# Attention with two heads per quarter of 32 partitions, score products on four row tiles, and five batches in flight

## The chip, the cores and the metric

The kernel runs on one core of one Trainium2 chip. The core has five engines that run their own instruction streams: TensorE (PE, products; its weight loads are shown as PEld), VectorE (DVE), ScalarE (ACT), GpSimd (POOL) and SyncE (SP, which here only starts DMAs). They meet at semaphores. The metric is the device time of one execution of the whole program in microseconds, the median of the runs; lower is better.

## The reference, cut to what matters

The program is a small audio tower over 64 sequences of 256 x 128: a convolution to tokens (64 x 248 x 64), an attention layer, a feed-forward layer on the top half of the tokens, a recurrent layer with fast weights, and a layer of experts. The change is in the attention layer, which for each batch of 248 tokens and 64 channels computes, with 8 heads of 8 channels:

```python
q, k = heads of x @ Wqk.T;  v = heads of x @ Wv.T
patch = softmax(einsum('bhnd,bhmd->bhnm', q, k) * 8 ** -0.5)
pos   = softmax(rel(n, m) @ Wpos.T + bpos)          # the same for every batch
attn  = (1 - sigmoid(gating)) * patch + sigmoid(gating) * pos
out   = (attn / attn.sum(-1)) @ v
h_att = h_tok + heads joined(out) @ Wproj.T + bproj
```

x is the normed h_tok. Both are scratch tensors in HBM, of 64 x 124 x 2 x 64 floats.

## The kernel before, in words

`attention_layer` (line 250) first sets up its constants, among them `rt`, the 8 position softmaxes (lines 363 to 366, 493 to 496 and 532 to 549). Then every engine runs a loop over the 64 batches, one batch per iteration, with the first and last batch written out. The order on each engine is the order in the code; `Loop` (line 21) turns a named event of batch n into a value of a semaphore.

The 248 tokens stand as two halves of 124 (TL) on partitions. A batch goes like this on TensorE:

- Eight score products (line 438). All 64 channels of q are the weights (124 tokens) and `ka` holds, for each head, the keys with all other heads' channels set to zero, two heads per product: 496 moving columns. VectorE takes the maximum over the keys of each (line 615). The scores use two banks in turn, so product i waits for maximum i-2. Between them stand three parts of the batch before: its sums are turned (line 414) and VectorE normalizes them (lines 586 to 599), the attended values are turned (421) and projected (427), and VectorE adds h_tok (610).
- The weighted sums of the position weights (line 393 with `rt`): per head 32 output partitions, so four heads share the array as column tiles of 32.
- The maxima are turned into rows (line 449) and VectorE copies them, negated, under the queries (`qa`, line 624): the maximum is subtracted by the product itself, by 8 extra rows of `ka` that pick the head.
- Eight times two turned score products (line 458): keys are the weights, `qa` moves, 248 columns each, all 128 rows in use. ScalarE takes the exponential (line 506) into `ex`. Again two banks, so head h waits for exponential h-2.
- The next batch's x is turned (373), copied by VectorE (558), multiplied to queries and keys (378); VectorE scales the queries (561) and spreads the keys over the heads (565: 64 partitions x 1984 elements). ScalarE copies the queries (509).
- The weighted sums of `ex` (line 393 again; line 392 waits for one exponential ahead of each product of the first half), then the values of the next batch (383). VectorE copies the sums (634) and the values (569). The next batch's score products wait for that last copy (line 432).

SP loads x and h_tok of a batch and stores its result (lines 330 to 354), each with one buffer. All of it is fp32; each product runs as two passes, which are two records in the trace.

Elsewhere in the kernel, the recurrent layer has other products in tiles. Line 2277 multiplies 32 rows by 128 columns, alternating two quarters of the rows and two banks, and the full products of line 2290 and the column tiles of lines 2303 and 2310 follow it. Their code is:

```python
for w in range(2):
    for k in range(2):
        rows = slice(32 * g, 32 * g + 32)          # g differs with k
        mm = e.matmul(psNew[X % 2][k][:, HD * w:HD * w + HD], wy[rows, ...], hist[rows, m * 4 + j, 0:HD], start=True, stop=True)
```

Of the kernel before, what the change touches and what calls it, by code (L numbers as in the profile page):

```python
# [7 lines left out]
ALU = mybir.AluOpType  # L8
ACT = mybir.ActivationFunctionType
AX = mybir.AxisListType.X  # L10
# [239 lines left out]
def attention_layer(nc, Wqk, Wv, Wpos, bpos, Wproj, bproj, gating, H0, X0, H1):  # L250
# [5 lines left out]
    with ExitStack() as ctx:  # L256
# [3 lines left out]
        wT = S.sb("wT", [D + 1, 4, D])  # L260
        prm = S.sb("prm", [TL, 40])
        hm = S.sb("hm", [D, NH])
# [5 lines left out]
        xT = S.sb("xT", [D, L])  # L268
# [3 lines left out]
        mx = S.sb("mx", [TL, 2, NH])  # L272
        ex = S.sb("ex", [TL, NH, 2, L])
# [6 lines left out]
        V = Loop(S.sem("vector"), [f"mx{i}" for i in range(8)] + ["nm", "xT", "q", "k", "evs", "v"])  # L280
        VE = Loop(S.sem("vector_end"), ["rz", "rzg", "num", "rv", "sum", "rd", "at0", "at1", "aT", "h1"])
        A = Loop(S.sem("scalar"), ["rvs"] + [f"e{h}" for h in range(NH)] + ["qc"])
        T = Loop(S.sem("tensor"), [f"s{i}" for i in range(8)] + ["rv", "nm"] + [f"st{h}" for h in range(NH)] +
                 ["xT", "qk", "ev", "v"])
        TE = Loop(S.sem("tensor_end"), ["te", "tr", "aT", "pr"])
        xin = Loop(S.sem("x_in"), ["x"], 16, 0)
        s_x0, s_t0, s_v0, s_a0 = S.sem("first_x_in"), S.sem("first_tensor"), S.sem("first_vector"), S.sem("first_scalar")
        hin = Loop(S.sem("h_in"), ["h"], 16, 0)
        out = Loop(S.sem("out"), ["h"], 16, 0)
        with nc.Block() as block:  # L290
            @block.gpsimd
            def _(e):
# [3 lines left out]
                e.memset(hm[:, :], 1.0).then_inc(s_id, 1)  # L296
                e.wait_ge(s_id, 3)
                e.memset(ka[D:, :, :], 1.0).then_inc(s_id, 1)
                e.wait_ge(s_id, 4)
                e.memset(va[:, :, :, :], 0.0).then_inc(s_id, 1)  # L300
                e.wait_ge(s_id, 5)

                e.affine_select(out=hm[:, :], in_=hm[:, :], compare_op=ALU.is_ge, fill=0.0, base=0,
                                pattern=[[-8, NH]], channel_multiplier=1).then_inc(s_id, 1)
                e.wait_ge(s_id, 6)
                e.affine_select(out=hm[:, :], in_=hm[:, :], compare_op=ALU.is_ge, fill=0.0, base=7,
# [15 lines left out]
            def _(e):  # L322
# [11 lines left out]
                def store(n):  # L334
                    VE.wait(e, n, "h1")
                    settled(e, s_own_sp)
                    e.dma_start(row(H1, n), h1[:, :, :]).then_inc(out.sem, 16)
# [2324 lines left out]
```

## Time and profile before

| | |
|---|---|
| median of 3 runs | 11612.14 us (11609.99 to 11624.89) |
| the profiled execution | 11640.99 us |
| its span, first to last instruction | 11639.3 us |
| mean granted TensorE clock over the span | 0.872 |
| PE busy, share of the span | 9361.1 us, 80% |
| DVE busy | 4926.0 us, 42% |
| ACT busy | 1971.5 us, 17% |

The granted clock is a fraction of 2.4 GHz. An engine is busy while one of its instructions runs; products are pipelined, their records overlap, and so the start of one record to the start of the next tells more than their lengths. "Idle before" is the time in which an engine had nothing to run ahead of a group, and what ended it. Numbers of one profiled execution are not the times of the unprofiled runs: here the former is 28.85 us longer than the median.

### The profile page before, as it was taken

How to read it: one execution, taken by the hardware profiler on the slowest of the kernel's cores; microseconds unless marked ns; L12 is line 12 of the kernel's file. 1: busy time of each engine (PE TensorE's matmuls, PEld its weight loads, DVE VectorE, ACT ScalarE, POOL GpSimd, SP SyncE). 2: the span in 40 equal slices, each digit the busy share in tenths (PEclk: the TensorE clock that was granted, in tenths of full speed). 3: DMA queues.
4: the chain of work that ended last, by engine and by line, in shares of the span. 5: the costliest groups of instructions: out<-in, count | busy, mean ns of one | idle time of the engine just before them, and what ended most of it. 6: DMA issues, size and time to landing. Idle time of an engine off the chain costs nothing. (4 is left out here: it accounts for less than half of the span.)

```text
span 11639.3 us, 367698 instructions
## 1 busy us (share of the span) xinstructions
PE 9361.1 (80%) x150364; PEld 5949.8 (51%) x150364; DVE 4926.0 (42%) x12504; ACT 1971.5 (17%) x4398; POOL 232.7 (2%) x167
## 2 busy tenths in 40 slices
PE   5788886242568988988989988989889898986777
PEld 2455553112346766666666666657566575652222
DVE  3444444544744344334344343333333333335555
ACT  1222221122111011011011011110111101113333
POOL 0000000000100000000000000000000000000000
PEclk8899998555889989989999989879789797887888
DMA  2000000142621011011021011120221202210000
GB/s 58 6 8 8 7 8 15 37 131 41 123 74 57 19 56 57 19 56 57 19 57 56 20 56 57 49 86 19 86 60 46 86 20 85 64 43 12 11 11 10
DMA packets 894544, 521.49 MB, mean 45 GB/s; under 512 B 379950, under 2 KB 889462, under 8 KB 892534
## 3 DMA queue, kind: packets, MB, share of 16 engines
q1 hardware_dynamic: 880694, 502.37, 15.9%
q0 software_dynamic: 13312, 12.57, 0.6%
q8 instruction: 262, 4.29, 0.2%
q14 instruction: 276, 2.26, 0.1%
HBM read 323.24 MB, written 154.20 MB: 41 GB/s over the span
## 5 line engine op out<-in xcount | busy, mean ns | idle before, releaser
L2344 PE MATMUL bank<-mv,hdiag 128*32 128x144 f32 x63744 | 2082.2, 289 | 9.8 <-DVE hdiag L2513 8.3
L2344 PEld LDWEIGHTS bank<-mv,hdiag 128*32 128x32 f32 x63744 | 1954.0, 111 | 95.1 <-DVE hdiag L2513 12.3
L2379 PE MATMUL bank<-mvt,ydiag 128*32 128x256 f32 x31872 | 1955.2, 381 | 0.0
L2379 PEld LDWEIGHTS bank<-mvt,ydiag 128*32 128x32 f32 x31872 | 1086.5, 110 | 533.6 <-issue 2.9
L438 PE MATMUL att_bank<-att_ka,att_qn 128*124 128x496 f32 x1024 | 496.2, 597 | 133.6 <-DVE att_mx L615 67.0
L2545 DVE TENSOR_TENSOR rep<-bank,ta 128x128 f32<-128x128 f32 x249 | 72.7, 292 | 1220.5 <-PE bank L2344 1220.5
L2223 ACT ACTIVATE work<-work 128x128 f32<-128x128 f32 x498 | 154.1, 309 | 2413.9 <-DVE work L2503 2413.9
L2468 DVE SCALAR_TENSOR_TENSOR mvt<-mvt,cu,bank 128x256 f32<-128x256 f32 x512 | 223.2, 477 | 741.6 <-PE bank L2277 741.6
L2277 PE MATMUL bank<-hist,wy 32*128 32x256 f32 x2048 | 399.6, 559 | 169.4 <-DVE wy L2458 169.4
L2211 ACT ACTIVATE mv<-bank 128x256 f32<-128x256 f32 x1024 | 325.1, 385 | 1100.7 <-PE bank L2290 1100.5
L458 PE MATMUL att_bank<-att_qa,att_ka 128*124 128x248 f32 x2048 | 464.6, 385 | 32.6 <-DVE att_qa L624 32.6
L1554 DVE TENSOR_TENSOR moe_hw<-moe_hb,moe_bank 128x496 f32<-128x496 f32 x512 | 326.2, 669 | 323.6 <-ACT moe_hb L1413 297.0
L2290 PE MATMUL bank<-r_ident,mvt 128*128 128x128 f32 x2048 | 404.2, 362 | 34.7 <-DVE mvt L2476 34.0
L2576 DVE TENSOR_SCALAR work<-bank,ta 128x128 f32<-128x128 f32 x498 | 174.9, 351 | 591.7 <-PE bank L2379 591.7
L458 PEld LDWEIGHTS att_bank<-att_qa,att_ka 128*124 128x124 f32 x2048 | 345.9, 186 | 144.3 <-DVE att_qa L624 48.8
L1335 PE MATMUL moe_bank<-moe_x,moe_w 128*128 128x496 bf16 x1536 | 412.4, 412 | 0.0
L2277 PEld LDWEIGHTS bank<-hist,wy 32*128 32x128 f32 x2048 | 232.5, 264 | 349.3 <-issue 248.2
L615 DVE TENSOR_REDUCE att_mx<-att_bank 124x2 f32<-124x496 f32 x512 | 339.0, 672 | 166.5 <-PE att_bank L438 162.7
L2290 PEld LDWEIGHTS bank<-r_ident,mvt 128*128 128x128 f32 x2048 | 320.8, 187 | 168.5 <-issue 99.9
L2310 PE MATMUL bank<-hdiag,ct 128*32 128x256 f32 x2944 | 317.8, 542 | 108.7 <-DMA hdiag<-between_slopes 108.7
L1413 ACT ACTIVATE moe_hb<-moe_bank,moe_b1s 128x496 f32<-128x496 f32 x512 | 328.7, 670 | 268.1 <-PE moe_bank L1335 262.2
L506 ACT ACTIVATE att_ex<-att_bank 124x496 f32<-124x496 f32 x512 | 298.5, 583 | 223.3 <-PE att_bank L458 223.3
(402 smaller groups left out, 10682.5 us busy)
## 6 DMA issues: line engine op xcount, KB each, us to landing
hdiag<-between_slopes SPq DMA_DIRECT2D x368, 512.0 KB, 4.7
baset<-between_base SPq DMA_DIRECT2D x265, 128.0 KB, 2.1
between_base<-work SPq DMA_DIRECT2D x256, 128.0 KB
hist<-h SPq DMA_DIRECT2D x1992, 8.0 KB
hist<-y SPq DMA_DIRECT2D x1992, 2.0 KB
hist<-dl SPq DMA_DIRECT2D x1992, 8.0 KB
ct<-between_table SPq DMA_DIRECT2D x184, 128.0 KB, 3.7
between_slopes<-key_zero SPq DMA_DIRECT2D x8, 2048.0 KB
```

The costliest lines, as they stand in the source:

```text
L438: e.matmul(bank[3 + i % 2][0:TL, 0:2 * L], qn[:, TL * a:TL * a + TL], ka[:, 2 * hp:2 * hp + 2, :], start=True, stop=True).then_inc(T.sem, 1)
L458: mm = e.matmul(bank[3 + h % 2][0:TL, L * mh:L * mh + L], ka[:, h, TL * mh:TL * mh + TL], qa[:, :], start=True, stop=True)
L615: e.tensor_reduce(mx[:, i // 4, 2 * (i % 4):2 * (i % 4) + 2], bank[3 + i % 2][0:TL, 0:2 * L].rearrange("p (h m) -> p h m", h=2), AX, ALU.m ...
L1335: mm = e.matmul(bank[2 + 2 * a + q][:, 0:2 * L], w[:, x_, 128 * a:128 * a + 128], xp[:, 2 * L * q:2 * L * q + 2 * L], start=(k == 0), stop ...
L1413: e.activation(hb[:, a, q, :], bank[2 + 2 * a + q][:, 0:2 * L], ACT.Relu, bias=b1s[:, x_, a:a + 1]).then_inc(A.sem, 1)
L1554: e.tensor_tensor(hw[:, a, q, :], hb[:, a, q, :], bank[q][:, 0:2 * L], ALU.mult).then_inc(V.sem, 1)
L2211: e.activation(dst, src, ACT.Copy).then_inc(A.sem, 1)
L2277: mm = e.matmul(psNew[X % 2][k][:, HD * w:HD * w + HD], wy[rows, G % 2, w, :, :].rearrange("p u d -> p (u d)"), hist[rows, m * 4 + j, 0:HD ...
L2290: mm = e.transpose(psC[k][:, o:o + 128], mvt[:, 4 * n + j, HD * w + 128 * hf:HD * w + 128 * hf + 128], ident[:, :])
L2310: mm = e.matmul(out[rows, :], ct[:, yk % 2, 1 + k, g % 2, rows], ring[xk % DX][:, j, :], start=False, stop=(k == nb - 1))
L2344: mm = e.matmul(psP[32 * j:32 * j + 32, 0:MW], hdiag[:, hf, r, j, :], mv1[:, hf, r, j, :], start=(hf == 0 and r == 0), stop=(hf == 1 and r ...
L2379: mm = e.matmul(psBack[hf][32 * j:32 * j + 32, :], ydiag[:, n, j, :], both, start=(n == 0), stop=(n == 7))
```

## The change: what it does

The layout of the heads changes. Partitions 32g to 32g+32 (a quarter) now hold heads 2g and 2g+1: 16 rows of channels, then 2 rows for the two maxima. The weights for queries and keys (`wqk`) are spread to this layout in the setup, with a row of ones for the maxima's rows of the keys, so queries and keys come out of one product each with 128 outputs. `ka` holds for each quarter the keys of its first and its second head, 2 x 248 columns on 128 partitions. A score product uses the 32 rows of one quarter as weights and moving data; so does a turned one. The maxima are written to where a transposing product brings them under the right rows, and VectorE forms `qa` by one subtraction.

Score product i goes to quarter i mod 4 and banks 0 and 1; the turned products of step i use quarter (i + 2) mod 4 and banks 2 and 3 (`TILE_HEAD` gives the head).

The order changes. There is one body, a turn k, of eight steps. In it: the scores and maxima of batch k+1, the turned scores and exponentials of k, the weighted sums of k-1 (in steps 4 to 7), the sums' turning and normalizing of k-2, the end of k-3, and x, queries, keys of k+2 with their values at the end of the turn. `qn`, `ka`, `va` and `ex` have three buffers. The loop holds three turns and runs 19 times; turns -2 to 2 and 60 to 66 are written out, without the parts whose batch does not exist. ScalarE takes over the copies of the sums, the values, x and the attended values. Each stage has a semaphore of its own.

```diff
-        qn, qa, ka = S.sb("qn", [128, L]), S.sb("qa", [128, L]), S.sb("ka", [128, NH, L])
-        va = S.sb("va", [TL, 2, NH, 32])
+        qn, ka = S.sb("qn", [128, 3, L]), S.sb("ka", [128, 3, 2, L])
+        qa = S.sb("qa", [128, L])
+        va = S.sb("va", [TL, 3, 2, NH, 32])
+        mx = S.sb("mx", [TL, 2, 128])
+        ex = S.sb("ex", [TL, 3, NH, 2, L])
...
+        TILE_HEAD = [2 * ((i + 2) % 4) + i // 4 for i in range(8)]
...
+        def turns(e, body):
+            for k in range(-2, 3):
+                body(Turn(k, k % 3))
+            with e.Fori(0, 19) as m:
+                for u in range(3):
+                    body(Turn(3 * m + (3 + u), u))
+            for k in range(60, B + 3):
+                body(Turn(k, k % 3))
...
+                def score(t, i):
+                    a, g = i // 4, i % 4
+                    rows = slice(32 * g, 32 * g + 32)
+                    if i == 0:
+                        t.wait(e, V_in, 1, "ka")
+                    t.wait(e, V_max, 1 if i >= 2 else 0, f"mx{(i - 2) % 8}")
+                    e.matmul(bank[i % 2][0:TL, 0:2 * L], qn[rows, t.buf(1), TL * a:TL * a + TL], ka[rows, t.buf(1), :, :],
+                             start=True, stop=True).then_inc(T_max.sem, 1)
+
+                def score_turned(t, i):
+                    h = TILE_HEAD[i]
+                    rows = slice(32 * (h // 2), 32 * (h // 2) + 32)
+                    if i == 0:
+                        t.wait(e, V_max, 0, "qa")
+                    t.wait(e, A_exp, 0 if i >= 2 else -1, f"e{(i - 2) % 8}")
+                    for mh in range(2):
+                        mm = e.matmul(bank[2 + i % 2][0:TL, L * mh:L * mh + L], ka[rows, t.buf(0), h % 2, TL * mh:TL * mh + TL], qa[rows, :],
+                                      start=True, stop=True)
+                    mm.then_inc(T_exp.sem, 1)
+
+                def turn(t):
+                    for i in range(8):
+                        if t.has(1):
+                            score(t, i)
+                        if t.has(0):
+                            score_turned(t, i)
+                        if i == 0 and t.has(-3):
...
+                                mm = e.transpose(bank[5][0:D, TL * a:TL * a + TL], at[:, a, :], ident[0:TL, 0:TL])
...
+                        if i == 1 and t.has(-2):
+                            t.wait(e, A_sum, -2, "evs")
+                            turned(t, evs, bank[6], "te")
+                        if i == 2 and t.has(-2):
+                            t.wait(e, A_sum, -2, "rvs")
+                            turned(t, rvs, bank[7], "tr")
+                        if i == 2 and t.has(2):
...
+                                mm = e.transpose(bank[5][0:D, TL * a:TL * a + TL], xn[:, a, :], ident[0:TL, 0:TL])
...
+                        if i == 3 and t.has(-3):
...
+                                mm = e.matmul(bank[5][0:TL, 256 + D * a:256 + D * a + D], aT[:, TL * a:TL * a + TL], wT[:, 1, :], start=True, stop=True)
...
+                        if i == 4 and t.has(2):
...
+                                mm = e.matmul(bank[4][:, L * w:L * w + L], wqk[:, w, :], xT[:, :], start=True, stop=True)
...
+                        if t.has(-1):
+                            if i == 4:
...
+                                weighted(t, ex[:, t.buf(-1), :, :, :], bank[6], 0, 0)
+                            if i == 5:
+                                weighted(t, ex[:, t.buf(-1), :, :, :], bank[6], 0, 1)
+                                weighted(t, ex[:, t.buf(-1), :, :, :], bank[6], 1, 0)
+                            if i == 6:
+                                weighted(t, ex[:, t.buf(-1), :, :, :], bank[6], 1, 1).then_inc(T_sum.sem, 1)
+                                weighted(t, rt, bank[7], 0, 0)
+                            if i == 7:
...
+                    if t.has(1):
+                        t.wait(e, V_out, -3, "h1")
+                        t.wait(e, V_max, 1, "mx7")
...
+                            mm = e.matmul(bank[5][:, TL * a:TL * a + TL], mx[:, a, :], ident[0:TL, 0:TL], start=True, stop=True)
...
+                    if t.has(2):
+                        t.wait(e, V_in, 2, "ka")
...
+                            mm = e.matmul(bank[4][0:TL, D * a:D * a + D], xT[0:D, TL * a:TL * a + TL], wT[0:D, 0, :], start=True, stop=True)
...
+                            e.activation(ex[:, t.buf(0), TILE_HEAD[i], :, :], bank[2 + i % 2][0:TL, 0:2 * L].rearrange("p (m n) -> p m n", m=2),
+                                         ACT.Exp).then_inc(A_exp.sem, 1)
...
+                            e.tensor_tensor(ka[:, t.buf(2), :, :], bank[4][:, L:2 * L].unsqueeze(1).to_broadcast([128, 2, L]),
+                                            hm[:, :].unsqueeze(2).to_broadcast([128, 2, L]), ALU.mult).then_inc(V_in.sem, 1)
...
+                        t.wait(e, T_max, 1, "nm")
+                        e.tensor_tensor(qa[:, :], qn[:, t.buf(1), :], bank[5][:, 0:L], ALU.subtract).then_inc(V_max.sem, 1)
```

On ScalarE step i has the exponential of the turned product i of batch k; step 0 also the copy of the `ex` sums (`evs`) of k-2, step 1 those of the `rt` sums (`rvs`), of the attended values of k-3 (`aT`) and of the values of k+1 (`va`), step 2 that of x of k+2 (`xT`). On VectorE a turn has the eight maxima, the eight normalizing operations of k-2 spread over steps 2 to 6, the residual sum of k-3 and the scaled queries of k+2 in step 4, the keys of k+2 in step 5, and at the end `qa`. On SP a turn loads x of k+3 once TensorE has turned that of k+2, stores the result of k-3 and loads h_tok of k-2.

## Rows read from the trace of the kernel before

**Rows 1.** The page, first line: the span.
```profile
span 11639.3 us, 367698 instructions
```
**Rows 2.** Busy time by stretch (instructions): PE, PEld, DVE, ACT, POOL, granted clock, DMA share, GB/s.
```profile
1001.20:1501.20 500.00, 436.19 (x2801) 259.66 (x2801) 234.84 (x480) 113.14 (x200) 0.00 (x0) 1.00 0.03 8
1957.00:2500.00 543.00, 196.32 (x450) 74.61 (x450) 293.40 (x524) 105.39 (x179) 0.79 (x3) 0.54 0.14 38
```
**Rows 3.** Timeline of the attention layer: start, length in us, engine, line, operation.
```profile
345.06 0.17 DVE L553 TENSOR_SCALAR att_omg<-att_prm 124x8 f32<-124x8 f32 x1
...
1001.20 1.93 PE L438 MATMUL att_bank<-att_ka,att_qn 128*124 128x496 f32 x4 [1.03 <-DVE att_va L569]
...
1026.20 1.93 PE L438 MATMUL att_bank<-att_ka,att_qn 128*124 128x496 f32 x4 [1.03 <-DVE att_va L569]
...
1953.93 0.29 DVE L610 TENSOR_TENSOR att_h<-att_bank,att_ht 124x128 f32<-124x128 f32 x1 [0.94 <-PE att_bank L427]
```
**Rows 4.** Timeline of TensorE inside one batch.
```profile
1003.40 0.60 PE L414 MATMUL att_bank<-att_ident,att_rvs 128*124 128x128 f32 x4
1003.84 1.83 PE L438 MATMUL att_bank<-att_ka,att_qn 128*124 128x496 f32 x4
...
1022.72 1.88 PE L393 MATMUL att_bank<-att_ex,att_va 124*32 124x248 f32 x32
1024.53 0.64 PE L383 MATMUL att_bank<-att_wT,att_xT 64*124 64x64 f32 x4
```
**Rows 5.** Groups by line, 1001.2 to 1501.2 us: busy us, mean ns, idle before.
```profile
L458 PEld LDWEIGHTS att_bank<-att_qa,att_ka 128*124 128x124 f32 x640 | 108.1, 186 | 45.1 <-DVE att_qa L624 15.8 <-ACT att_ex L506 13.7
...
L438 PEld LDWEIGHTS att_bank<-att_ka,att_qn 128*124 128x124 f32 x321 | 50.7, 186 | 90.6 <-DVE att_mx L615 47.8 <-DVE att_va L569 24.5 <-issue 18.3
L565 DVE TENSOR_TENSOR att_ka<-att_bank,att_hm 64x1984 f32<-64x1984 f32 x20 | 44.1, 2205 | 0.0
...
L634 DVE COPY att_evs<-att_bank 128x496 f32<-128x496 f32 x20 | 13.1, 656 | 0.0
...
L503 ACT ACTIVATE att_rvs<-att_bank 128x496 f32<-128x496 f32 x20 | 11.7, 583 | 283.4 <-PE att_bank L393 283.4
...
L509 ACT ACTIVATE att_qa<-att_qn 64x248 f32<-64x248 f32 x20 | 8.2, 410 | 33.7 <-DVE att_qn L561 33.7
L558 DVE COPY att_xT<-att_bank 64x248 f32<-64x248 f32 x20 | 8.2, 408 | 151.3 <-PE att_bank L373 151.3
...
L569 DVE COPY att_va<-att_bank 124x128 f32<-124x128 f32 x20 | 5.5, 273 | 0.0
```
**Rows 6.** Timeline: 3287.90 to 3287.95 (first row), then 3287.9 to 3290.6.
```profile
3287.90 0.48 PE L2277 MATMUL bank<-hist,wy 32*128 32x256 f32 x2
...
3287.90 1.13 PE L2277 MATMUL bank<-hist,wy 32*128 32x256 f32 x8
3288.97 1.09 PE L2290 MATMUL bank<-r_ident,mvt 128*128 128x128 f32 x8
```
**Rows 7.** Timeline of TensorE from 1022.716 to 1022.740: 24 ns.
```profile
1022.72 0.42 PE L393 MATMUL att_bank<-att_ex,att_va 124*32 124x248 f32 x4
```
**Rows 8.** Timeline of TensorE, 3288.66 on and 3289.57 on.
```profile
3288.44 0.59 PE L2277 MATMUL bank<-hist,wy 32*128 32x256 f32 x4
...
3289.57 0.49 PE L2290 MATMUL bank<-r_ident,mvt 128*128 128x128 f32 x3
3289.99 0.42 PE L2303 MATMUL bank<-w,ct 64*32 64x256 f32 x4
```
**Rows 9.** Timeline of VectorE in the first batch.
```profile
357.26 0.68 DVE L615 TENSOR_REDUCE att_mx<-att_bank 124x2 f32<-124x496 f32 x1 [0.16 <-PE att_bank L438]
...
359.12 0.68 DVE L615 TENSOR_REDUCE att_mx<-att_bank 124x2 f32<-124x496 f32 x1 [0.16 <-PE att_bank L438]
```
**Rows 10.** Busy time by stretch, columns as in rows 2.
```profile
345.00:352.00 7.00, 4.09 (x11) 2.30 (x12) 3.37 (x8) 0.41 (x1) 0.00 (x0) 0.50 0.06 18
3287.90:3300.00 12.10, 10.64 (x108) 6.22 (x104) 8.01 (x20) 4.83 (x14) 0.00 (x0) 1.00 0.76 233
```

More of the change, by code:

```diff
@@ L286, in attention_layer, with stage @@
[L286 to L289, printed above, removed]
+        def stage(name, names, unit=1):
+            return Loop(S.sem(name), names, unit, 0)
+        V_in = stage("vector_in", ["qn", "ka"])
+        V_max = stage("vector_max", [f"mx{i}" for i in range(8)] + ["qa"])
+        V_att = stage("vector_att", ["rz", "rzg", "rv", "num", "sum", "rd", "at0", "at1"])
@@ new lines, in attention_layer, with __init__, has, n @@
+        T_att = stage("tensor_att", ["te", "tr"])
+        T_out = stage("tensor_out", ["aT", "pr"])
+        xin, hin, out = stage("x_in", ["x"], 16), stage("h_in", ["h"], 16), stage("out", ["h"], 16)
+        TILE_HEAD = [2 * ((i + 2) % 4) + i // 4 for i in range(8)]
+        class Turn:
+            def __init__(self, k, third):
+                self.k, self.third, self.fixed = k, third, isinstance(k, int)
+            def has(self, d):
+                return not self.fixed or 0 <= self.k + d < B
+            def n(self, d):
+                return self.k + d
+            def buf(self, d):
+                return (self.third + d) % 3
+            def wait(self, e, loop, d, name):
+                if self.has(d):
+                    loop.wait(e, self.k + d, name)
@@ L381, in values @@
-                def values():
-                    for a in range(2):
-                        mm = e.matmul(bank[4][0:TL, D * a:D * a + D], xT[:, TL * a:TL * a + TL], wT[0:D, 2, :], start=True, stop=True)
-                    return mm
-                def weighted(wts, bk, exps):
-                    for g in range(2):
-                        for mh in range(2):
-                            for j in range(4):
-                                if exps is not None and mh == 0:
-                                    A.wait(e, exps, f"e{4 * g + j}")
-                                mm = e.matmul(bk[32 * j:32 * j + 32, L * g:L * g + L], va[:, mh, 4 * g + j, :], wts[:, 4 * g + j, mh, :],
-                                              start=(mh == 0), stop=(mh == 1))
-                    return mm
@@ L479, in _, with weighted @@
-                batch(0, True, False)
-                with e.Fori(1, B - 1) as n:
-                    batch(n, True, True)
-                batch(B - 1, False, True)
-                end_turned(B - 1)
-                end_attended(B - 1)
-                end_projected(B - 1)
+                e.wait_ge(s_v, 107)
+                def weighted(t, wts, bk, g, mh):
+                    for j in range(4):
+                        mm = e.matmul(bk[32 * j:32 * j + 32, L * g:L * g + L], va[:, t.buf(-1), mh, 4 * g + j, :], wts[:, 4 * g + j, mh, :],
+                                      start=(mh == 0), stop=(mh == 1))
+                    return mm
@@ L487, in _ @@
+                turns(e, turn)
             @block.scalar
             def _(e):
-                e.nop().then_inc(A.sem, A.P)
                 e.wait_ge(s_w, 16 * 7)
@@ L516, in _ @@
+                turns(e, turn)
             @block.vector
             def _(e):
[L518 to L522 removed]
                 e.wait_ge(s_t, 3)
                 e.wait_ge(s_w, 16 * 7)
[L525 removed]
+                e.memset(wqk[:, :, :], 0.0).then_inc(s_v, 1)
@@ L650, in ffn_layer @@
+                turns(e, turn)
 def ffn_layer(nc, wr, br, w1, b1, w2, b2, H1, H2, XN, WD, SW):
```

375 lines of the change are left out of this document (153 added, 222 removed).

## The prediction

> **What bounds the kernel now.** I read the page first, then busy time by stage, then one batch of the attention layer in order of time, and last two places elsewhere in the kernel where TensorE already works in tiles.
>
> The change touches the attention layer alone. The first attention instruction after the setup follows 345.06 us, and the last residual sum starts at 1953.93 us [rows 3]: 1609 us for 64 batches, 14% of the span [rows 1]. In the middle, equal work recurs at 1001.20 and 1026.20 us [rows 3], so a batch takes 25.0 us. In twenty batches (500 us) TensorE is busy 436, VectorE 235, ScalarE 113 us, and the granted clock is 1.00, the 2.4 GHz level [rows 2]. TensorE leads, but by engine busy time it is pipelined records that overlap, so I count pitches (start to start) instead. A score pass of 496 columns: (1.83 - 0.579)/3 = 0.417 us. A pass of 248 columns: the 32-record group of weighted sums runs four column tiles at once, so (1.88 - 0.375)/7 = 0.215, say 0.21. The transposes: (0.60 - 0.273)/3 = 0.109 [rows 4]. A product has two passes (16 records for 8 score products a batch).
>
> Per batch: scores 16 x 0.417 = 6.7; turned scores 32 x 0.21 = 6.7; weighted sums 16 groups of four x 0.21 = 3.4; transposes of the sums 8 x 0.109 = 0.9; x and attended transposes 4 x 0.11 = 0.4; queries and keys 4 x 0.21 = 0.8; values 4 passes at (0.64 - 0.27)/3 = 0.12, projection and maxima likewise (an estimate) = 1.4. Sum 20.3 us. The other 4.7 us are waits, and the rows of the weight loads name them [rows 5]: per batch 2.4 us for maxima, 1.2 us for the values' copy at the head of a batch, 0.8 us for the maxima's copy into the queries, 0.7 us for exponentials. A batch is a chain: maxima must be complete before its turned scores, and those before the next batch's queries and keys may enter the same banks.
>
> **The change, part by part.**
>
> *Row tiles.* Two heads live in each 32 partitions, so a score product reads only rows 32g to 32g+32, and the turned one of the same step reads quarter g+2 and writes another pair of banks. Do two such products run at once? In the recurrent stage L2277 has exactly this form (32*128, 256 columns, alternating quarters and banks). Two of its records start within the same 50 ns, and from the first of eight to the next group, at 3288.97, it is 1.07 us, where one after another they would need 8 x 0.213 = 1.7 (0.109 per 128 columns, scaled) [rows 6]. So two run at the price of one. What if a semaphore wait stands between them, as here? L393 on the exponentials waits separately before each of four column tiles (line 392), and still four start within 24 ns [rows 7]; as there are two passes per product, the second passes come after. I take full overlap: a step costs the longer of 2 x 0.417 and 4 x 0.21, 0.84 us, eight steps 6.7 instead of 13.4. Saved: 6.7 us per batch. Bounds: nothing and 6.7.
>
> The Trainium skill, "TensorE: Matmul & The Clock Gate", section "Measured speedup vs the span model", says MATMULs start and end strictly in program order. Under that rule the turned product could begin only with the score product's second pass. L393's four near-simultaneous starts, with two passes each, speak against it.
>
> *Everything else on TensorE* keeps its count and pitch. The maxima are now turned by a 128-column product, queries and keys are 128 outputs wide; both still four passes. I keep 13.6 us of products per turn (20.3 - 6.7).
>
> *Changes of tiling.* New: every step of row tiles is followed by work in another tiling. A change costs: from L2277's last pair at 3288.44 + 0.22 to the full-array L2290 at 3288.97 it is 0.31 instead of 0.215, and from L2290's last at 3289.57 + 2 x 0.109 to L2303 0.20 instead of 0.109 [rows 8]: 0.1 us each. Per turn I count steps 0 to 3 two changes each, step 4 three, steps 5 and 6 two, step 7 with maxima and values four: 19, so 1.9 us. Bounds 0 (hidden behind loads) and 0.2 each, 3.8.
>
> *Waits.* Five batches in flight: in turn k the scores are of k+1, turned scores of k, weighted sums of k-1, the end of k-2 and k-3, queries and keys of k+2. Nearly every operand is a turn old. What remains inside a turn: step i needs maxima and exponentials of i-2. A pair of steps with its other products lasts at least 2.5 us on TensorE, and the way from one score over its maxima to the next use of its bank took 1.86 us in batch 0, where nothing else stood between (maxima 2 steps apart at 357.26 and 359.12, [rows 9]). The exceptions: the turned scores' first needs the copy made from the maxima turned at the end of the turn before (a record of 0.27 and a copy of 0.41 us, mostly under the values and score 0: 0.2), and the transposes of the sums need ScalarE's two 0.58 us operations after step 0 (0.2). A load that comes late costs 0.1 (the first four score records, after a wait, take 1.93, later ones 1.83; [rows 3, 4]); with a few of these I take 0.7 us per turn, bounds 0 and 4.7 (all of today's).
>
> *VectorE* gives away the copies of sums, values, x and attended (13.1 + 5.5 + 8.2 and, of the same shape, 8.2 us in twenty batches) and the keys' product shrinks from 1984 to 496 columns (2.2 to about 0.6): 235 - 35 - 44 + 12 = 168, or 8.4 us a turn. *ScalarE* gains 0.58 + 0.41 + 0.41 + 0.27 and loses 0.41: 5.66 + 1.3 = 6.9 us [rows 2, 5]. Neither reaches TensorE, so both edits cost nothing while TensorE needs over 9; if they lose that cover the turn is theirs. ScalarE's four operations in step 1 (1.8 us) delay exponential 2, which TensorE wants only in step 4. SP: x, sums and h stay one load or store each per turn, issued a turn ahead of use; xn and ht keep one buffer, but have a turn (over 13 us) to land. Setup gains some seven short VectorE operations: 2 us. The loop now has three turns per branch; I give that nothing.
>
> *Sum.* 13.6 + 1.9 + 0.7 = 16.2 us per turn. 64 turns, and one more for filling and emptying (69 thinner turns): 64 x 16.2 + 16 + 2 = 1055 us instead of 1609, so 554 less. The profiled execution took 11640.99 us, its span 11639.3; it would be 11087. The three timed runs have their median at 11612.14, 29 lower than the profiled one, and I subtract the same 554: **11058 us**.
>
> **The rivals.**
>
> *A, in-order starts.* The second passes do hold the queue, a step costs 0.417 + 0.84: 3.3 us more per turn, 19.5, or 1270 us: 11273. Against it, rows 7; for it, that no row has a semaphore release and a wait between two row tiles.
>
> *B, hand-overs.* The tiles overlap, but each step pays for its waits as today's turned products do for exponentials (13.7 us in twenty batches of three such waits, 0.23 each, [rows 5]), plus 0.1 for the load behind: 0.3 x 8 = 2.4 more, 18.6 per turn, 1211 us: 11214. Against it: those results are a whole step older now.
>
> *C, no overlap at all.* 20.3 + 1.9 + 0.7 = 22.9, or 1490 us: 11493. Against it rows 6; for it, that there 256 columns stand on both sides, here 496 beside 248.
>
> *D, slower than before: the clock.* TensorE is at 0.50, its 1.2 GHz level, at the head of the attention loop [rows 10] and at 0.54 in the next stage, where it is busy 36% [rows 2]. If products on a quarter of the rows leave it there, 13.6 doubles: 27.2 + 1.9 = 29.1 per turn, 1893 us: 11896. It decides from some 25 us per turn. Against it: right after 3287.90, with L2277 and narrow tiles in the mix, the clock is 1.00 [rows 10].
>
> **How the numbers follow.** Forecast 0.62, A 0.12, B 0.12, C 0.09, D 0.05. The forecast's own range: turns of 15.2 (changes cheaper, no waits) to 17.6 give 10993 to 11149. A and B lie inside 11300; C and D are left out with the tail below: low 10985, high 11300. A measurement here can tell 0.2%, 23 us, from no change. All but D are faster by far: faster 0.94, same 0.01, slower 0.05.
>
> **What would show it.** Score and turned-score records of different quarters that start within some 10 ns of each other, and a period of about 16 us in the timeline: right. The first turned record 0.4 us behind the score's: A. Idle weight loads released by maxima and exponentials in most steps: B. A period over 22 us at clock 1.00: C. A granted clock near 0.5 in the attention stage: D. The tilings' price shows as 0.3 us from the last 248-column pass of a step to the next full-array record. The forecast is wrong if the turn is outside 15 to 18 us, if VectorE or ScalarE becomes the one that others wait for, or if another stage moves by more than 20 us.

## The result

The changed kernel takes 11138.33 us (median of 4, 11126.18 to 11155.73) where the kernel before takes 11618.51 us (median of 4): a ratio of 0.9587, 95% interval 0.9572 to 0.9602. That is 480 us less; the forecast was 554 less (11058 us, range 10985 to 11300). The sign and the place were right. The profiled execution took 11155.73 us where the sum had 11087, so 69 us have to be explained.

The page of the changed kernel: span, granted clock in 40 slices (of 279 us each), and the two products with the maxima and exponentials that they feed (last columns: busy us, mean ns, idle before and who ended it).
```profile
span 11154.1 us, 367656 instructions
PEclk8799965558999899999999997988979788788888
L431 PE MATMUL att_bank<-att_qa,att_ka 32*124 32x248 f32 x2048 | 583.0, 411 | 0.5 <-DVE att_qa L645 0.5
L421 PE MATMUL att_bank<-att_ka,att_qn 32*124 32x496 f32 x1024 | 577.0, 661 | 3.7 <-DVE att_mx L606 3.7
L606 DVE TENSOR_REDUCE att_mx<-att_bank 124x2 f32<-124x496 f32 x512 | 344.9, 675 | 491.1 <-PE att_bank L421 491.1
L525 ACT ACTIVATE att_ex<-att_bank 124x496 f32<-124x496 f32 x512 | 298.6, 584 | 711.3 <-PE att_bank L431 702.6
```
Against [rows 5]: TensorE now waits 4.2 us in the whole stage for maxima and their copy, VectorE and ScalarE wait 491 and 703 us for TensorE. TensorE bounds this stage alone.

Timeline of the changed kernel: the end of the attention setup, a turn's first product after the sums (the turned maxima, L499) and its first two steps, the same product one and three turns later, and the last residual sum.
```profile
346.45 0.17 DVE L592 TENSOR_SCALAR att_omg<-att_prm 124x8 f32<-124x8 f32 x1
...
800.37 0.37 PE L499 MATMUL att_bank<-att_ident,att_mx 124*128 124x124 f32 x1
...
801.58 0.68 PE L421 MATMUL att_bank<-att_ka,att_qn 32*124 32x496 f32 x1
801.66 0.67 PE L431 MATMUL att_bank<-att_qa,att_ka 32*124 32x248 f32 x2
802.09 0.57 PE L421 MATMUL att_bank<-att_ka,att_qn 32*124 32x496 f32 x1
802.17 0.58 PE L431 MATMUL att_bank<-att_qa,att_ka 32*124 32x248 f32 x2
802.68 0.40 PE L446 MATMUL att_bank<-att_ident,att_at 124*64 124x124 f32 x2
...
803.01 0.68 PE L421 MATMUL att_bank<-att_ka,att_qn 32*124 32x496 f32 x1
803.02 0.47 PE L431 MATMUL att_bank<-att_qa,att_ka 32*124 32x248 f32 x1
...
817.13 0.37 PE L499 MATMUL att_bank<-att_ident,att_mx 124*128 124x124 f32 x1
...
856.99 0.37 PE L499 MATMUL att_bank<-att_ident,att_mx 124*128 124x124 f32 x1
...
1499.16 0.29 DVE L625 TENSOR_TENSOR att_h<-att_bank,att_ht 124x128 f32<-124x128 f32 x1 [2.66 <-DMA att_ht<-between_h_tok]
```
The stage lasts 1499.16 - 346.45 = 1152.7 us where it lasted 1608.9 [rows 3]: 456 of the 485 us between the two profiled executions. A turn is 817.13 - 800.37 = 16.76 us. The two products of a step start 10 to 80 ns apart: they do run at once. But from 817.13 to 856.99 there are 39.86 us for two turns, not 33.5.

Busy time of the changed kernel by stretch (columns as in rows 2): the head of the loop, the rest of it, and inside it one ordinary turn and a piece of a slow one.
```profile
345.00:410.00 65.00, 55.91 (x224) 29.41 (x224) 21.59 (x44) 10.73 (x23) 0.00 (x0) 0.50 0.02 5
410.00:1499.00 1089.00, 1083.70 (x8739) 660.77 (x8737) 507.56 (x1245) 399.08 (x809) 0.00 (x0) 0.96 0.04 11
800.37:817.13 16.76, 16.76 (x145) 10.36 (x141) 8.23 (x20) 6.41 (x13) 0.00 (x0) 1.00 0.04 11
826.70:840.40 13.70, 13.70 (x85) 6.08 (x84) 3.73 (x10) 1.75 (x3) 0.00 (x0) 0.50 0.03 9
```
This is what the forecast didn't have. The granted clock stays at 0.50, the 1.2 GHz level, until 410 us (before it rose at 356), and it falls to it again six times, five times for 13.7 us and, while the pipeline empties, once for 23.9, though TensorE's records leave no gap: busy 13.70 of 13.70 us in the fall shown. Before, it was 1.00 in the loop [rows 2]. A fall of 13.7 us adds 6.3 us to its turn (39.86 - 2 x 16.76). In all 156 us of the stage are at the lower level, where it was 11.

The rest of the kernel, after the attention layer, takes 30 us less than before, nearly all of it in the recurrent layer, whose code is the same: 7201 us before and 7171 now, from the start of its first instruction to that of its last.

### The profile page after: what moved, and what is told of

Its sections match the earlier page's. It is cut to its first block and busy times, and to the rows that moved or that the text cites. A ratio compares the mean times of both kernels' runs of the same rounds, so it can differ in the third digit from the quotient of the medians.

```text
span 11154.1 us, 367656 instructions
## 1 busy us (share of the span) xinstructions
PE 9070.6 (81%) x150364; PEld 5786.7 (52%) x150364; DVE 4704.4 (42%) x12252; ACT 2018.2 (18%) x4590; POOL 230.5 (2%) x167
## 3 DMA queue, kind: packets, MB, share of 16 engines
q14 instruction: 241, 1.97, 0.1%
## 5 line engine op out<-in xcount | busy, mean ns | idle before, releaser
L431 PE MATMUL att_bank<-att_qa,att_ka 32*124 32x248 f32 x2048 | 583.0, 411 | 0.5 <-DVE att_qa L645 0.5
L421 PE MATMUL att_bank<-att_ka,att_qn 32*124 32x496 f32 x1024 | 577.0, 661 | 3.7 <-DVE att_mx L606 3.7
L2277 PE MATMUL bank<-hist,wy 32*128 32x256 f32 x2048 | 396.6, 553 | 192.9 <-DVE wy L2458 192.9
L2277 PEld LDWEIGHTS bank<-hist,wy 32*128 32x128 f32 x2048 | 232.8, 261 | 370.4 <-issue 266.0
L431 PEld LDWEIGHTS att_bank<-att_qa,att_ka 32*124 32x124 f32 x2048 | 345.0, 190 | 34.8 <-issue 1.8
```

The lines of the kernel that those rows point to most:

```text
L421: e.matmul(bank[i % 2][0:TL, 0:2 * L], qn[rows, t.buf(1), TL * a:TL * a + TL], ka[rows, t.buf(1), :, :], start=True, stop=True).then_inc(T ...
L431: mm = e.matmul(bank[2 + i % 2][0:TL, L * mh:L * mh + L], ka[rows, t.buf(0), h % 2, TL * mh:TL * mh + TL], qa[rows, :], start=True, stop=True)
```

## The experiments

All were timed beside the kernel before. Each group of runs had its own pace (before: 11593.52 us for the first four, 11618.89 for the next four, 11607.16 for the last three), so the ratios are the measure; the times are medians.

**All rows.** The pipeline of five batches alone, with no row tiles. The kernel leaves out the separation of the heads: every score is a sum over the heads of all four quarters.
```diff
-                    rows = slice(32 * g, 32 * g + 32)
+                    rows = slice(0, 128)
...
-                    rows = slice(32 * (h // 2), 32 * (h // 2) + 32)
+                    rows = slice(0, 128)
```


> Score and turned products read all 128 partitions instead of one quarter, so every score sums over all heads of its set (that part of the computation is changed). Columns, passes and waits are those of the changed kernel. Theory 1: no overlap, 6.7 us more per turn, but 9 of 19 changes of tiling are gone; if each costs 0.16 us (0.09 until the next group, and a first record that is 0.05 to 0.1 longer) that is 1.4 us less: 22.0 us per turn, 338 us more than the changed kernel, 11475 us. If a change costs 0.1 as forecast: 22.6 us, 11510. Theory 2 on the clock: with all rows in use it stays at 1.00 from some 10 us after the head of the loop on, no falls. Rival (chance or fixed times): falls of 13.7 us every 160 us again.

Measured: 11389.36 us, ratio 0.9834 (0.9804 to 0.9864); a turn 21.81 us where 22.0 was expected, the clock up at 358 us and not down again until the stage's last half microsecond. Over 25.0 us before, the pipeline is worth 3.2 us per turn; row tiles are worth the 5.05 from there to 16.76. Four tenths of a turn's gain are waits that are gone, six tenths the tiles, with what their changes of tiling cost already taken off.

**Same quarter.** Both products of a step in one quarter of the rows, so that they can't overlap.
```diff
-        TILE_HEAD = [2 * ((i + 2) % 4) + i // 4 for i in range(8)]
+        TILE_HEAD = [2 * (i % 4) + i // 4 for i in range(8)]
```


> The turned products of step i go to the quarter that score product i uses (i mod 4 instead of (i + 2) mod 4); order, waits and changes of tiling stay. Theory 1 (the overlap of two quarters is what the change gains on TensorE): the two products of a step run one after the other, 8 x 0.84 = 6.7 us more per turn, so 23.4 instead of 16.76 us at clock 1.00, 64 x 6.7 = 430 us more than the changed kernel: about 11570 us. Rival (the gain is that of the missing waits alone): no difference, 11140. Theory 2 on the clock (products on few rows are what lets the granted clock fall): with one quarter at a time the clock in the attention loop lies clearly under the changed kernel's 0.93, down to 0.50 and then a turn of up to 45 us (over 12500 us). Rival (falls come by chance or at fixed times): about 0.93 again.

Measured: 12699.52 us, ratio 1.0968 (1.0935 to 1.1001), slower than before. Of the 2729 us of its stage 2627 are at the lower level, and a turn takes 41.3 to 44.2 us. One step of it, and one of the changed kernel at the same level, each with the start of the group behind it:
```profile
901.95 2.01 PE L421 MATMUL att_bank<-att_ka,att_qn 32*124 32x496 f32 x2
903.75 1.86 PE L431 MATMUL att_bank<-att_qa,att_ka 32*124 32x248 f32 x4
905.54 0.78 PE L475 MATMUL att_bank<-att_xT,att_wqk 65*128 65x248 f32 x1
```
```profile
397.18 1.18 PE L421 MATMUL att_bank<-att_ka,att_qn 32*124 32x496 f32 x1
397.19 1.19 PE L431 MATMUL att_bank<-att_qa,att_ka 32*124 32x248 f32 x2
...
399.13 0.64 PE L405 MATMUL att_bank<-att_ex,att_va 124*32 124x248 f32 x4
```
In one quarter the turned products begin when the score product's two passes are through, and the step takes 3.59 us where the changed kernel's takes 1.95. Both theories hold: without two quarters there is no overlap, and with fewer rows in use the clock is lower.

**Halves.** As the changed kernel, but a product reads the half of the rows that holds its quarter; what the kernel leaves out is again the separation of the heads (the scores are sums over four).
```diff
-                    rows = slice(32 * g, 32 * g + 32)
+                    rows = slice(64 * (g // 2), 64 * (g // 2) + 64)
...
-                    rows = slice(32 * (h // 2), 32 * (h // 2) + 32)
+                    rows = slice(64 * (h // 4), 64 * (h // 4) + 64)
```


> The changed kernel, but each product for scores reads 64 partitions (the half that holds its quarter) where it read 32; what it computes is the sum over four heads instead of two. Number, width and order of the products stay, and the two products of a step still lie in different halves, so they can overlap as before. Clock theory (the granted clock falls, and rises late, because products that use a quarter of the rows keep TensorE too lightly used although its records are without a gap): the turn at full clock stays 16.8 us, the clock rises at some 358 us instead of 410 and has fewer falls or none, and the time is lower than the changed kernel's by what 155 us at the lower level cost: each fall cost 6.3 us of turn, six and the head some 60 us together, so 11060 to 11085 us. Rival 1 (the falls come from something else that the change brought: the waits, the order of work): clock rows as in the changed kernel, 0.93 in the same stretches, and 11110 to 11150 us. Rival 2 (two halves don't overlap as quarters do): a turn above 18 us, and over 11200 us.

Measured: 11086.99 us, ratio 0.9545 (0.9521 to 0.957); turns of 16.77 to 16.79 us without exception, the clock up at 372 us and no fall in the loop. The profiled execution is 75 us faster than that of the changed kernel with the same turn; its attention stage is 57 us shorter (1096.1 and 1152.7 us), and that is the clock. The other 18 us are outside the stage.

The same stretch, 400 to 1200 us, of four kernels (columns as in rows 2), in this order: same quarter, changed kernel, halves, all rows.
```profile
400.00:1200.00 800.00, 800.00 (x2652) 407.51 (x2652) 155.89 (x372) 122.04 (x249) 0.00 (x0) 0.52 0.02 4
```
```profile
400.00:1200.00 800.00, 798.41 (x6438) 485.89 (x6434) 377.61 (x916) 293.96 (x597) 0.00 (x0) 0.96 0.04 11
```
```profile
400.00:1200.00 800.00, 800.00 (x6691) 498.94 (x6690) 392.80 (x957) 304.62 (x618) 0.00 (x0) 1.00 0.04 11
```
```profile
400.00:1200.00 800.00, 800.00 (x5122) 501.57 (x5122) 304.14 (x735) 235.33 (x478) 0.00 (x0) 1.00 0.03 9
```
TensorE is busy all the time in all four, but for 1.6 us in the second. What differs is how many rows are in use at once in the score products: 32, 64 by two quarters, 128 by two halves, 128. The granted clock follows that and not the busy time. The Trainium skill, "TensorE: Matmul & The Clock Gate", section "What's actually happening", says that the gate goes by how busy the array has been recently; these rows show that a busy engine in the profile is not enough.

**Pairs.** Two steps at once: scores i and i+1, then turned i and i+1, in four different quarters.
```diff
-                        if t.has(1):
-                            score(t, i)
-                        if t.has(0):
-                            score_turned(t, i)
+                        if i % 2 == 0:
+                            for s in (i, i + 1):
+                                if t.has(1):
+                                    score(t, s)
+                            for s in (i, i + 1):
+                                if t.has(0):
+                                    score_turned(t, s)
```


> Two steps' row tiles stand together: scores i and i+1, turned products i and i+1, and then what followed each. Four quarters are in use at once, and there are 11 changes of tiling per turn instead of 19. Theory 1: TensorE needs 4 x 0.84 instead of 8 x 0.84, and 8 x 0.16 us less for tilings: 16.76 - 3.4 - 1.3 = 12.1 us; the first two pairs must wait for two maxima (0.2 + 2 x 0.675 after the scores), so 12.3 to 13.0 us per turn, 240 to 285 us less than the changed kernel: 10855 to 10900. Rival A (weight loads of four quarters go one after the other, 12 x 0.104 = 1.25 per pair): 1.6 us more, 13.9 to 14.6 per turn, 10960 to 11000. Rival B (the maxima's and exponentials' waits take all back, as the older result is now one pair away): 16 us or more, no gain. Clock: theory 2 gives more rows in use at a time, so fewer falls than in the changed kernel.

Measured: 10913.55 us, ratio 0.9424 (0.9399 to 0.945), a turn of 13.91 us. Timeline of TensorE in this kernel, the third pair of a turn and the group behind it:
```profile
800.50 0.68 PE L421 MATMUL att_bank<-att_ka,att_qn 32*124 32x496 f32 x2
800.51 0.69 PE L431 MATMUL att_bank<-att_qa,att_ka 32*124 32x248 f32 x4
801.01 0.58 PE L421 MATMUL att_bank<-att_ka,att_qn 32*124 32x496 f32 x2
801.03 0.59 PE L431 MATMUL att_bank<-att_qa,att_ka 32*124 32x248 f32 x4
801.55 1.10 PE L478 MATMUL att_bank<-att_xT,att_wqk 65*128 65x248 f32 x4
```
Four products take 1.05 us from the first record to the next group, where a step of two took 802.68 - 801.58 = 1.10. So the loads do not go one after another, and the rival's reason is refuted although its turn came out. What kept the turn at 13.91 are waits, 1.3 us a turn, which stand in this kernel's waits of TensorE (700 to 1200 us: total, times, longest):
```profile
PE att_bank L412 <- ACT att_evs L533: 26.2, 35, 0.8
PE att_bank L471 <- ACT att_xT L550: 19.9, 36, 0.6
```
In the middle of its loop, with four quarters in use, the clock doesn't fall: 1.00 from 409 to 1255 us. Its scores are the changed kernel's own, so it doesn't take the other values of halves and all rows for the clock to hold.

**Pairs, same quarters.** The same with the other TILE_HEAD, so that four products share two quarters.

> As the pairs kernel, but each turned product in the quarter of its score product, so two quarters at a time as in the changed kernel, and only the number of changes of tiling per turn differs from it, 11 instead of 19. If a change costs 0.16 us: 1.3 us less, 15.5 us per turn, 83 us less than the changed kernel, 11055. At 0.1 us: 16.0, 11090. At 0.2: 15.2, 11035. If waits grow by more than that: no faster than 11138.

Measured: 11313.47 us, ratio 0.9769 (0.974 to 0.9799). The expectation missed twice. First, at full clock the turn is 17.4 us, not 15.5. One pair of steps with the start of the group behind it, and this kernel's waits of TensorE (700 to 1200 us, 23 turns):
```profile
904.25 1.10 PE L421 MATMUL att_bank<-att_ka,att_qn 32*124 32x496 f32 x4
905.19 1.10 PE L431 MATMUL att_bank<-att_qa,att_ka 32*124 32x248 f32 x8
906.22 0.63 PE L405 MATMUL att_bank<-att_ex,att_va 124*32 124x248 f32 x8
```
```profile
PE att_bank L412 <- ACT att_evs L533: 17.0, 23, 0.8
PE att_bank L471 <- ACT att_xT L550: 12.7, 23, 0.6
```
Scores and turned products of one quarter go one behind the other, 1.97 us for four, where two steps of the changed kernel take 2.2. The two waits of the pairs kernel take back 1.3 us a turn; the other 0.6 us of the miss stays open. Second, 498 us of the stage are at the lower clock, most of them in falls of 17 to 24 us. The stretch from 400 to 1200 us, first of the pairs kernel, then of this one:
```profile
400.00:1200.00 800.00, 725.93 (x8027) 474.15 (x8019) 446.56 (x1143) 339.69 (x742) 0.00 (x0) 1.00 0.05 14
```
```profile
400.00:1200.00 800.00, 751.26 (x5316) 446.48 (x5315) 300.77 (x756) 226.36 (x494) 0.00 (x0) 0.81 0.03 9
```
The kernel with the less busy TensorE and four quarters keeps the clock. But two quarters at once gave 0.96 in the changed kernel and 0.81 here, so the rows in use at once are not all: the order of the products counts as well, and how is open.

**Early copies.** Pairs, and ScalarE copies both sums ahead of the turn's first exponential, which lets the transposes of the sums start at once.
```diff
-                        if t.has(0):
-                            t.wait(e, T_exp, 0, f"st{i}")
...
                         if i == 0 and t.has(-2):
                             t.wait(e, T_sum, -2, "ev")
...
-                        if i == 1 and t.has(-2):
+                        if i == 0 and t.has(-2):
                             t.wait(e, T_sum, -2, "rv")
...
+                        if t.has(0):
+                            t.wait(e, T_exp, 0, f"st{i}")
```


> The pairs kernel with one more edit: ScalarE makes both copies of the sums (evs, rvs) at the start of its turn, ahead of the first exponential, where before they stood behind the first and the second. In the pairs kernel's trace TensorE stood from some 809.95 to 810.81 us in a turn ahead of the first transpose of evs: the copy was queued behind an exponential that itself waits for the second product of the pair. Theory (that wait is the whole of what the pairs kernel lost against its forecast of 12.3 to 13.0 us per turn): the turn is 13.91 - 0.8 = 13.1 us, 64 turns give back 52 us, and the time is 10865 us; more than 10890 would speak against it. Rival (something else is next, the exponentials being late by the two copies of 0.58 us that now stand before them): the turn stays at 13.6 to 14.0 us and the time at 10895 to 10920.

Measured: 10919.71 us, ratio 0.9406 (0.9382 to 0.9431), a turn of 13.61 us, the rival's. The wait for evs is gone from the trace, but the second pair now comes before its maxima: only 0.3 of the 0.8 us came back, and by the time alone it can't be told from the pairs kernel.

**Next input first.** That, with the transposes of x ahead of those of the relative sums.
```diff
-                        if i == 2 and t.has(-2):
-                            t.wait(e, A_sum, -2, "rvs")
-                            turned(t, rvs, bank[7], "tr")
                         if i == 2 and t.has(2):
...
+                        if i == 2 and t.has(-2):
+                            t.wait(e, A_sum, -2, "rvs")
+                            turned(t, rvs, bank[7], "tr")
```


> The pairs kernel with early copies and one more edit: after the second pair of steps TensorE turns the layer's next input first and the relative sums second, where it was the other way round. In the trace of that kernel TensorE stood 0.55 us per turn ahead of the projection, for ScalarE's copy of the turned input; the four transposes of the relative sums (0.65 us) now lie over that copy. Theory: the turn is 13.61 - 0.5 = 13.1 us, 64 turns give 32 us, ratio to the kernel before 0.938 (10885 to 10895 us by this chip's earlier pace). Rival (VectorE's maxima are next: the third pair of steps waits for them longer): 13.4 to 13.6 us per turn and a ratio of 0.940 to 0.941.

Measured: 10883.63 us, ratio 0.9385 (0.9367 to 0.9404), a turn of 13.16 us, as the theory said. TensorE waits for the copy (L471 on L550) 0.6 us from 700 to 1200 us, where it was 20.4 with early copies alone. By the time alone the two can't be told apart either (their intervals overlap); the turn tells them apart.

**Grouped sums.** The changed kernel with all weighted sums in step 7 instead of steps 4 to 7.
```diff
-                            if i == 4:
+                            if i == 7:
                                 t.wait(e, A_exp, -1, "e7")
...
+                                for g, mh in ((0, 0), (0, 1), (1, 0)):
+                                    weighted(t, ex[:, t.buf(-1), :, :, :], bank[6], g, mh)
```


> The changed kernel with its sums (the 64 column-tile products of 0.209 us streams) all in step 7 of the turn instead of spread over steps 4 to 7. It takes away three entries into column tiles and three returns to row tiles per turn, and nothing else. Theory (a change of tiling costs 0.13 to 0.19 us, 3.0 us per turn for 19): the turn is 16.76 - 6 x 0.16 = 15.8 us, 64 turns give 61 us, and the time is 11070 us at the changed kernel's share of low clock. By the forecast's price of 0.1 us the turn is 16.16 us and the time 11095. Rival (with the steps 4 to 7 back to back, VectorE, which has its longest work there, comes late and TensorE waits): a turn of 16.8 us or more and 11130 us or more. If the bare row-tile steps let the clock fall more often, turns of 23 us show it.

Measured: 11093.22 us, ratio 0.9549 (0.9528 to 0.957), a turn of 16.22 us. Its waits of TensorE, 700 to 1200 us:
```profile
PE att_bank L421 <- DVE att_mx L601: 22.8, 31, 0.7
```
So 0.74 us of each turn are a new wait, the rival's. If it is counted in full, the six changes of tiling gave 0.54 + 0.74 = 1.28 us, 0.21 each, and a change is dearer than the forecast's 0.1; the turn alone is also what 0.1 each would give (16.16). The clock had five falls here too, of 7 to 14 us; 107 us of the stage are at the lower level, where the changed kernel has 156, and that is part of the gain.

**All three orders** (pairs, early copies, grouped sums).

> All three orders together: steps two by two, copies of the sums first on ScalarE, the sums' products in one block. If each keeps its price, the turn is 13.1 us less one entry and one return (steps 4-5 and 6-7 had two blocks, now one): 12.8 us, and 10845 us. Rival: eight steps in four blocks leave VectorE (8.4 us of work per turn by the forecast) only some 6 us between the first score and the last before the sums, so TensorE waits for it and the turn is 13.5 to 14.5 us: 10890 to 10950 us.

Measured: 10991.96 us, ratio 0.9461 (0.944 to 0.9481), a turn of 14.80 us, past even the rival's 14.5. The last two pairs stand back to back, and VectorE isn't done with the last pair's banks. The idle time of the scores' weight loads from 700 to 1200 us, first in the early-copies kernel (37 turns), then in this one (34), last columns as in rows 5:
```profile
L421 PEld LDWEIGHTS att_bank<-att_ka,att_qn 32*124 32x124 f32 x592 | 53.6, 179 | 32.1 <-DVE att_mx L609 26.8
```
```profile
L421 PEld LDWEIGHTS att_bank<-att_ka,att_qn 32*124 32x124 f32 x541 | 58.4, 179 | 55.5 <-DVE att_mx L604 50.6
```
Per turn they wait 1.5 us for maxima instead of 0.7. The sums spread over the steps were the cover of VectorE's work. Once, at 653 us, the clock falls here, for 3.4 us, with four quarters in use.

**Warm start.** Ten full products behind each of the setup's last eight pairs of transposes, in the changed kernel and in "next input first".
```diff
+                    if k >= 8:
+                        for _ in range(10):
+                            e.matmul(bank[7][:, 0:128], ident[:, :], ident[:, :], start=True, stop=True)
```


> The changed kernel with the same added products in its setup and nothing else. Clock theory: the loop starts at the upper level, so of the 64 us at the lower level at its head some 32 us come back: 11138 - 32 = 11105 us; the later falls of 13.7 us remain, since they come from the loop's own products. Rival (the head's low clock is set by the loop's products, two quarters at a time, and not by what came before): the clock falls within 20 us of the loop's start, and the time is 11125 to 11145 us.

> The same, and in the second half of the attention layer's setup TensorE also multiplies the identity by itself, ten products of 128x128 with 128 columns behind each of the last eight pairs of transposes, into a bank that nothing reads before it is written again. Clock theory: the granted clock is at its upper level before the loop starts (some 346 us) instead of at 398, so 52 us at the lower level become 26 us: 25 us less than without it. Rival (the quarter-row products that follow bring it down again at once): a fall within the first 20 us of the loop and less than 8 us gained, or the added products hold up the setup and the loop starts after 355 us.

Measured: 11158.97 us, ratio 0.9616 (0.96 to 0.9633), and 10860.8 us, ratio 0.9361 (0.9345 to 0.9377). Busy time by stretch of the first of them:
```profile
320.00:340.00 20.00, 15.59 (x133) 14.64 (x132) 12.46 (x34) 2.97 (x10) 0.00 (x0) 1.00 0.00 1
340.00:350.00 10.00, 7.31 (x44) 5.38 (x43) 3.31 (x16) 1.24 (x4) 0.00 (x0) 0.86 0.02 7
350.00:390.00 40.00, 34.55 (x122) 18.98 (x120) 14.98 (x25) 7.27 (x16) 0.00 (x0) 0.50 0.02 5
```
The rival is right on the clock. The products bring the clock up, with TensorE busy 15.59 of 20 us, and the loop's own first turns take it down again at 347 us, busy 34.55 of 40. The level at the head is set by those turns. Neither kernel gained by its time: each one's interval overlaps that of the kernel without the products. The attention stage came out 7 us shorter in the first (1146.1 us) and 1 us in the second (878.2 and 879.6), far from the 32 and 25 expected. The first kernel's ratio is even 0.3% above the changed kernel's, with intervals that just overlap, and its time is above both figures given; the cause is open.

The best order of those tried, "next input first", takes 10883.63 us: a ratio of 0.9385 to the kernel before, where the change has 0.9587.

## Why the prediction was right, and where its size was off

*Row tiles: right.* Two quarters run at once, also with waits between them. Rivals A and C are out: by the trace, with starts 10 to 80 ns apart, by the pairs, where even four do, and by the same quarter, where a step loses the overlap.

*Order of starts.* In the rows above the turned product's first pass starts at 801.66 us, ahead of the score product's second at 802.09, which stands before it in the program. The rule of the Trainium skill weighed in the forecast ("TensorE: Matmul & The Clock Gate"; it stands there in the section "The mechanism", not in the one that the forecast names) doesn't hold between different row tiles here, and the row of weighted sums was the better guide.

*Changes of tiling: the step that was mis-sized.* "0.1 us each", 1.9 us per turn. With products at 13.6 (the forecast's own count) and waits of 4.2 us / 64 = 0.07, 16.76 leaves 3.1 us for 19, or 0.16 each. The other runs put the price between 0.13 and 0.21: a step takes 1.10 us where its streams are 0.84, 0.13 for each of its two changes; all rows, which had no waits of TensorE from 700 to 1200 us, leave 21.81 - 20.3 = 1.5 us for ten, 0.15 each; the grouped sums say 0.21 for the six they remove. The forecast read a step's end and the next start, but not that the first record behind a change is itself longer: 0.68 us for L421's first pass above and 0.57 for its second. The 0.16 is within the bounds given (0 to 0.2 each). The Trainium skill, "TensorEngine Tiling (Array Packing)", section "Key Properties", says that changing the tiling mode drains the engine; it gives no price, and these are the estimates here.

*Waits: too high.* 0.7 us were taken and 0.07 found; rival B is out. The turn-old operands do what they were counted on for. The two misses are of opposite sign: 16.2 forecast, 16.76 measured, 36 us over 64 turns.

*The clock: left out of the forecast.* This is the larger part. Rival D had the mechanism and was priced as all or nothing, with a chance of 0.05: "it decides from some 25 us per turn". Whether it decides was the wrong question; it could also act in part. By the halves, with every product in place, it cost 57 us of the attention stage, and the two traces say where: five turns longer by 6.3 us are 31, the head (to the fourth L499) is 15 longer, and the end, from the last L499 on, with the fall of 23.9 us, is 11 longer (37.8 and 26.7). The halves too start with 26 us at half clock, so 57 is what the clock cost beyond that. With one quarter in use (same quarter) the clock did what D says, and at 41 to 44 us the turn was above D's 29.1, since without overlap the products are longer too. The evidence against D, rows 10, was of the recurrent layer, where eight L2277 are followed by eight full-array products [rows 6]. That the attention loop has fewer of those, and that this is the difference, is argued and not tested.

*VectorE and ScalarE: right.* They never bound the stage. In the loop VectorE's keys took 0.61 us and ScalarE's copies 0.58, 0.37 and 0.27.

*The other stages: wrong.* The forecast named 20 us as the most that another stage would move, and the recurrent layer moved by 30. In the eleven kernels tried its length lies between 7143 and 7184 us, 42 us apart with the same code, so much of the 30 may be scatter; why the one profiled execution of before lies above them all, at 7201, stays open.

*The sum.* 1055 us was forecast for the stage and 1153 measured, 98 more: 36 for the turn, 57 for the clock by the halves, and 5 for the setup, filling and emptying, in which the halves' own 26 us at half clock still are. With 30 off elsewhere that is the 69 us. That the total came within 1% is in part luck: the misses on waits and on the other stages went against those on tilings and clock.

## What to carry to other kernels

Row tiles in different quarters share TensorE even across waits, so issue as many quarters in a row as banks and buffers allow: four at once here cost no more than two, cut the changes of tiling from 19 to 11, and the clock held. Price every change of tiling at 0.13 to 0.21 us (an estimate from these runs), and look at the granted clock by stretch, since the busy share stays at 100% when it falls. Before work is grouped on the engine that bounds, ask which engine's work it was covering.

## What was not expected of the hardware

- The granted clock of a TensorE without a gap depended on the rows in use: no fall in the loop with 128 rows (two halves, all rows), six in the stage with two quarters, at the lower level for nearly the whole loop (0.52 in the stretch shown) with one. Four quarters, with gaps, kept it but for one fall of 3.4 us in one of the kernels. Two quarters in another order (pairs, same quarters) brought it to 0.81, so the rows alone don't settle it.
- With two quarters the clock fell from 1.00 to 0.50 within a few us of the loop's start, at 347 us, although full products had just run; it came back at 405, as late as in the changed kernel without them (410).
- Two score products and two turned ones (each two halves of 248 columns) in four different quarters take 1.05 us, no more than one of each in two quarters (1.10). Four in two quarters take 2.0.
